# Two groups of a block product share the matmul loop, and consecutive matmuls go to their two PSUM banks in turn

## Time and profile before

| | |
|---|---|
| median of 3 runs | 984.03 us (983.54 to 985.64) |
| the profiled execution | 983.49 us, of which its span in the profile is 981.7 us |
| TensorE matmuls (PE) | busy 976.0 us, 99% of the span, 4786 instructions |
| TensorE weight loads (PEld) | 806.6 us, 82% |
| VectorE (DVE) | 799.4 us, 81% |
| ScalarE (ACT) | 406.6 us, 41% |
| GpSimd (POOL) | 37.0 us, 4% |
| granted TensorE clock, mean | 0.999 |

### The profile page before, as it was taken

One profiled execution on the slowest core, in us unless ns is written; L12 is line 12 of the kernel. 1 busy time (PEld: TensorE's weight loads), 2 busy tenths in 40 slices (PEclk: granted clock), 3 DMA queues, 4 the chain that ended last, 5 costly groups with the idle time before them and its releaser, 6 DMA issues.

```text
span 981.7 us, 12530 instructions
## 1 busy us (share of the span) xinstructions
PE 976.0 (99%) x4786; PEld 806.6 (82%) x4786; DVE 799.4 (81%) x644; ACT 406.6 (41%) x373; POOL 37.0 (4%) x63
## 2 busy tenths in 40 slices
PE   9999999999999999999999999999999999999998
PEld 7888888888888888888898888888888888888886
DVE  3977877998967897778867788779987779897887
ACT  5553563443345333332355545444334453423312
POOL 2700000000000000000100000000000000000001
PEclk9999999999999999999999999999999999999999
DMA  9022035024112101240531210620340131012013
GB/s 351 15 86 108 1 134 208 18 70 169 48 44 96 76 1 65 81 177 0 189 155 42 87 43 6 229 109 25 119 158 1 43 129 44 1 64 86 1 44 129
DMA packets 23274, 84.69 MB, mean 86 GB/s; under 512 B 2722, under 2 KB 6834, under 8 KB 17330
## 3 DMA queue, kind: packets, MB, share of 16 engines
q1 hardware_dynamic: 20962, 76.03, 21.4%
q0 software_dynamic: 2112, 7.36, 1.9%
q10 hardware_dynamic: 144, 0.52, 0.2%
HBM read 75.51 MB, written 8.39 MB: 85 GB/s over the span
## 4 chain that ended last, share of the span: by engine, by line
PE 98%; DMA 1%; SPq 0%; DVE 0%; issue 0%
PE banks L697 31%; PE banks L698 31%; PE banks L699 31%; PE banks L789 2%; PE banks L753 1%; DMA r<-x_pairs_in 1%; PE banks L772 1%; SPq L549 0%; SPq L579 0%; PE banks L802 0%; PE banks L818 0%; DVE r L1089 0%; SPq L529 0%; PE banks L812 0%; SPq L504 0%
## 5 line engine op out<-in xcount | busy, mean ns | idle before, releaser
L697 PE MATMUL banks<-s_hi,t_hi 128*128 128x512 f32 x1344 | 525.4, 391 | 0.0
L698 PE MATMUL banks<-s_lo,t_hi 128*128 128x512 f32 x1344 | 523.1, 389 | 0.0
L699 PE MATMUL banks<-s_hi,t_lo 128*128 128x512 f32 x1344 | 523.0, 389 | 0.0
L697 PEld LDWEIGHTS banks<-s_hi,t_hi 128*128 128x128 f32 x1344 | 252.3, 188 | 54.6 <-issue 1.5
L699 PEld LDWEIGHTS banks<-s_hi,t_lo 128*128 128x128 f32 x1344 | 252.3, 188 | 52.6
L698 PEld LDWEIGHTS banks<-s_lo,t_hi 128*128 128x128 f32 x1344 | 252.4, 188 | 51.4
L958 DVE TENSOR_TENSOR t_lo<-w,t_hi 128x1024 fp32r<-128x1024 f32 x134 | 159.9, 1218 | 8.7 <-ACT t_hi L891 8.7
L1084 DVE TENSOR_TENSOR r<-banks,r 128x1024 f32<-128x1024 f32 x102 | 123.5, 1219 | 46.3 <-PE banks L699 39.8
L891 ACT CAST t_hi<-w 128x1024 fp32r<-128x1024 f32 x134 | 136.5, 1048 | 51.3 <-PE banks L699 42.3
L863 ACT CAST s_hi<-st 128x2048 fp32r<-128x2048 f32 x40 | 76.5, 1913 | 182.8 <-PE banks L699 130.4
L958 DVE TENSOR_TENSOR s_lo<-st,s_hi 128x2048 fp32r<-128x2048 f32 x40 | 91.6, 2291 | 46.0 <-ACT s_hi L863 46.0
(11 more groups left out here) (84 smaller groups left out, 428.2 us busy)
## 6 DMA issues: line engine op xcount, KB each, us to landing
w<-w_up_in SPq DMA_DIRECT2D x16, 1024.0 KB, 4.8
w<-w_base_in SPq DMA_DIRECT2D x10, 1024.0 KB, 4.9
w<-w_down_in SPq DMA_DIRECT2D x8, 1024.0 KB, 5.0
r<-x_t_in SPq DMA_DIRECT2D x8, 1024.0 KB, 6.3
w<-w_lin_in SPq DMA_DIRECT2D x8, 1024.0 KB, 5.2
out_t<-r POOLq DMA_DIRECT2D x14, 512.0 KB, 4.1
we<-w_expin_in SPq DMA_DIRECT2D x10, 512.0 KB, 4.6
r<-x_pairs_in SPq DMA_DIRECT2D x8, 512.0 KB, 9.8
```

Source lines behind the costliest of these rows:

```text
L697: pe.matmul(out, w_hi, x_hi, start=start, stop=False, skip_group_check=True)
L698: pe.matmul(out, w_hi, x_lo, start=False, stop=False, skip_group_check=True)
L699: return pe.matmul(out, w_lo, x_hi, start=False, stop=stop, skip_group_check=True)
```

## The change

Groups are taken in pairs (0, 1), (2, 3), (4, 5). Within a pair the loops run over chunks, over the three forms (0: hi*hi, 1: hi*lo, 2: lo*hi), and innermost over the two groups: consecutive matmuls use the same activation columns, other weights, and the two groups' banks in turn. The number of matmuls, their operands and, in each bank, their order stay as they were. All waits of the pair stand ahead of its first matmul: the bank of the odd group is waited for there too. The even group is signalled done by its last matmul, which is the last but one of the pair. The products of exp with i = 3, 4, 5 keep the old order. Nothing on the other engines is changed.

```diff
-            def product(n, g, p, start, stop):
+            def product(n, g, p, form, fresh):
                 out = banks[:, bank_of(n, g), :]
...
-                pe.matmul(out, w_hi, x_hi, start=start, stop=False, skip_group_check=True)
-                pe.matmul(out, w_hi, x_lo, start=False, stop=False, skip_group_check=True)
-                return pe.matmul(out, w_lo, x_hi, start=False, stop=stop, skip_group_check=True)
+                x = (s_lo if form == 1 else s_hi)[:, slot, cols]
+                return pe.matmul(out, w, x, start=fresh and form == 0, stop=form == 2 and p == chunks_in(n) - 1,
+                                 skip_group_check=True)
...
-                for g in range(groups_in(n)):
+                for first in range(0, groups_in(n), 2):
+                    pair = (first, first + 1)
+                    if kind == "exp" and i in (3, 4, 5):
+                        for g in pair:
+                            pe.wait_ge(s_ready, n + 1)
+                            pe.wait_ge(t_ready, t_at(n, t_half_of(n, g)))
+                            wait_bank_free(n, g)
+                            for p in range(chunks_in(n)):
+                                for form in range(3):
+                                    last = product(n, g, p, form, (g >= 4 or i == 5) and p == 0)
+                            last.then_inc(group_done, 1)
+                            route(n, g)
+                        continue
                     pe.wait_ge(s_ready, n + 1)
-                    pe.wait_ge(t_ready, t_at(n, t_half_of(n, g)))
-                    wait_bank_free(n, g)
-                    fresh = g >= 4 or i in (0, 1, 5)
-                    begun = lora and g >= 2
+                    pe.wait_ge(t_ready, t_at(n, t_half_of(n, first)))
+                    wait_bank_free(n, first)
+                    wait_bank_free(n, first + 1)
+                    fresh = first >= 4 or i in (0, 1, 5)
+                    begun = lora and first == 2
                     for p in range(chunks_in(n)):
-                        last = product(n, g, p, fresh and p == 0 and not begun, p == chunks_in(n) - 1)
-                    if lora and g == 1:
+                        for form in range(3):
+                            for g in pair:
+                                last = product(n, g, p, form, fresh and p == 0 and not begun)
+                                if p == chunks_in(n) - 1 and form == 2 and (not lora or first == 2):
+                                    last.then_inc(group_done, 1)
+                    if lora and first == 0:
                         pe.wait_ge(lora_ready, lora_count(n))
                         pe.wait_ge(t_ready, t_at(n, LORA))
                         wait_bank_free(n, 2)
                         wait_bank_free(n, 3)
                         lora_out(n)
-                    elif not lora or g >= 2:
-                        last.then_inc(group_done, 1)
-                    if kind == "exp":
-                        route(n, g)
```

More of the change, by code:

```diff
@@ L689, in tensor_engine @@
         def tensor_engine(pe):
-            def product(n, g, p, start, stop):
+            def product(n, g, p, form, fresh):
                 out = banks[:, bank_of(n, g), :]
                 at, slot = ((g * 2 if kind_of(n) == "expup" else g % 2 * 4) + p) * P, T_ID[n, t_half_of(n, g)] % 4
-                w_hi, w_lo = t_hi[:, slot, at:at + P], t_lo[:, slot, at:at + P]
+                w = (t_lo if form == 2 else t_hi)[:, slot, at:at + P]
                 slot, cols = s_place(n)
                 cols = slice(cols.start + p * TN, cols.start + (p + 1) * TN)
-                x_hi, x_lo = s_hi[:, slot, cols], s_lo[:, slot, cols]
-                pe.matmul(out, w_hi, x_hi, start=start, stop=False, skip_group_check=True)
-                pe.matmul(out, w_hi, x_lo, start=False, stop=False, skip_group_check=True)
-                return pe.matmul(out, w_lo, x_hi, start=False, stop=stop, skip_group_check=True)
+                x = (s_lo if form == 1 else s_hi)[:, slot, cols]
+                return pe.matmul(out, w, x, start=fresh and form == 0, stop=form == 2 and p == chunks_in(n) - 1,
+                                 skip_group_check=True)
             def wait_bank_free(n, g):
```

## The result

| | before | after |
|---|---|---|
| median us (22 runs each) | 983.43 (982.83 to 985.64) | 984.56 (983.77 to 988.25) |
| the profiled execution, us | 983.49, span 981.7 | 986.54, span 984.8 |
| DVE busy, us | 799.4 | 798.7 |

The ratio after to before is 1.0014, 95% interval 1.0008 to 1.0020: slower by 1.1 us, inside the forecast's "no change" of 0.2%. The forecast time is 0.04 us off, and that closeness is luck: the sum behind it left out about half of the loss, and started from a median that was 0.6 us too high, as will be seen. The profiled execution after the change is 2 us above its kernel's median, so a part of its span is not the change's.

A forecast was written before the change was run, and what follows sets the result against it. PE's own instruction chain bounds the kernel: 4032 matmuls at 226.7 ns, 914 of 981.7 us. Terms 0 + 0 + 0 + 0.6 us on 983.49 gave 984.1, plus 0.54 to the median: 984.6 us, range 982.9 to 986.6.

The forecast's parts named there:

- Banks in turn: Large matmuls on PE: alternating banks leaves the 226.7 ns spacing as it is; 0 us, bounds -48 and +23 us.
- Rival 1: Large matmuls: same-bank overhead of 13.4 ns is real and alternation lifts it; 48 us faster, 936 us; chance 0.05.
- rival 2: Large matmuls: alternation has a price per matmul, 6.3 ns at 233 ns spacing; +23 us, 1007 us; chance 0.04.
- Rival 3: PE's clock: gaps from alternation lower it to 1.2 GHz; a tenth of 3600 matmuls costs 77 us, 1061 us; chance 0.02.
- Weights changed at every matmul: Lines 697 and 698, neighbours sharing weights: separating them loses nothing, since the load is issued for 698 anyway; 0 us.
- Waiting for both banks ahead of the pair: Start of each pair: odd bank needed 2.7 us sooner (expup 1.4), covered by at least 5.4 - 2.7 us; 0 us.
- The even group is signalled 11 matmuls later: Readers of the even group: signal 2.5 us later (expup 1.1 us); sum +0.6 us, bounds +0.4 and +1.3.
- (a): "addb" and "gate" adds on DVE: second of a pair ends 0.65 us later, hidden; 16 us at the very worst.
- (b): LORA slot refill by ACT: starts about 2.5 us later, next s_lo slips about 1 us; lead 7.4 us, hidden.
- (c): Last product: group 3's add starts 0.42 us later behind group 2's, its store costs 0.2 us more.
- The tightest place: Expup, product 83: t_lo ends at 972.59, its matmul starts at 972.74; nothing moves, but there is no cover.
- Rival 4: Expup: uncovered DVE chain turns late, 0.65 us in each of five tight products, twice; 6.5 us, 991 us; chance 0.03.

The follow-up runs named there:

- m1: Changed kernel plus nine blocks of 48 matmuls behind the last product, varying banks, weights, width and type; some 100 us longer, spacing 226.7 ns in two and four banks.
- e1: Changed kernel with groups 2 and 3 of lin's product 6 one after the other as before; median 983.83 us, ratio 1.0008 to the kernel before.
- e5: Kernel before, old order; only in lin's product 6 is group 2 signalled together with group 3; median 984.30 us, ratio 1.0009 to the kernel before.
- e4: Kernel before, old order; even groups signalled together with the odd ones, except in exp's products 3, 4, 5; median 984.97 us, ratio 1.0017.

## Why the prediction was right, and where it was not

*Banks in turn, 0 ns: right.* The reading of the group borders in the earlier trace rows held for steady alternation: 16.32 us for 72 spacings, and m1 has the same spacing in one, two and four banks. Rival 1 (936 us) and rival 2 (1007 us) fell on that. The argument from the number of borders in two stages forecast it rightly, and m1 showed it. Rival 3 (the clock) fell as well: the granted clock was at its full level over the whole stream of large matmuls, and its one fall lay ahead of the first of them.

*The Trainium skill's figure* ("TensorE: Matmul & The Clock Gate", Back-to-back issue gap: N / 2.4 + 2.5 ns, 216 ns for 512 columns) is met by the bf16 blocks of m1, 216 ns, and not by the fp32r matmuls, 226.7 ns. The section calls it the gap of an isolated matmul and holds it for too large in a stream; in the streams of m1 the mean spacing is never below it. So the 10.9 ns that I weighed were there, but they go with the operands' type and not with the bank.

*Weights changed at every matmul, 0 us: right.* One block repeated 48 times is no faster than 32 different ones.

*Waiting for both banks ahead of the pair, 0 us: right where PE does not stand, as e1 shows, and 0.11 us short at each stall.* At the one place where PE did stand, both banks are freed by one add, so the wait ends at the same moment as in the old order; but the matmul starts 0.256 us after the add and not 0.147. That is 2 x 0.11 = 0.22 us of the loss. My cover, "at least 5.4 - 2.7 us", did not look at this place: before the change it was 2.4 us.

*The even group is signalled 11 matmuls later.* (a) "addb" and "gate": hidden, as said; no stall in up0, up1 or down. (b) **The refill of a LORA slot is the step that failed.** I wrote of DVE's next s_lo that it would "slip by about 1 us", against a lead of 7.4 us. That was one such slot, in the middle of lin, and there it came out as said: t_lo starts 2.47 us later, the 1.22 us that DVE idled behind it before the change are used up, the next s_lo is 1.17 us late, and no matmul waits. But I took this one slot for all and followed the lag no further. The slot of lin's product 6 is refilled for exp, where DVE goes 25 us without idle time over 0.11 us; a lag of 2.3 to 2.5 us travels through its list to an add on which PE depends with 2.4 us to spare. The term was 0.48 us, not 0; e1 and e5 show that this slot's signal opens the stall, and the second bank wait makes 0.22 us of it. (c) The last product: mechanism right, size 0.47 us against 0.6. The add came 0.38 us later (0.42 foreseen), and the store cost 0.1 us more, not 0.2.

*The tightest place*, did not move, as said.

*Sum.* 0.6 us predicted, from the tail alone; 0.95 us measured in the traces, 0.47 of tail and 0.48 of stall, and 0.9 to 1.1 us in the medians. So the loss was half as large again as forecast, or more. That the forecast time, 984.6 us, is so close to the measured 984.56 is luck: the median of the first three runs, from which it was reckoned, was itself 0.6 us above that of all 22, and this made up for the term left out. From 983.43 the same sum would have given 984.0. Rival 4 named the kind of thing that happened (a dependence turned late) but at the wrong place, in expup, and with more than ten times the price.

## What to carry to other kernels

Before alternating banks, look in the trace at the borders where the bank already changes: here two stages with different numbers of borders took the same time for the same matmuls, and there was nothing to win. When a group's end is signalled later, follow each waiter to where it acts and then down its engine's list as long as that has no idle time: here the lag was paid 25 us on. Count the waits in a row at such a place, since each takes time of its own once the engine stands. In the last group of a kernel keep results coming one after the other, since two that end together queue behind each other. And before a difference of two traces is put down to a change, compare the granted clock window by window.

## What the runs showed of the hardware

Adding to a bank just written costs nothing: 226.7 ns for 512 columns and 120 ns for 256, in one bank as in two (blocks of 48 matmuls). Over the columns at 2.4 GHz (213.3 and 106.7 ns) that is 13.3 ns for each fp32r matmul at either width, where bf16 has 2.5 ns. What in the 4-byte operands makes it was not taken apart; that weights of 64 columns are slightly slower (230 ns) than those of 128 speaks against the length of the weight load.

When PE stands for a bank that an add on DVE frees, the matmul starts 0.147 us after the add's end with one wait ahead of it (four stalls, e4 and e5) and 0.256 us with two (five of six stalls of the pair's order; the sixth 0.346).

In the start of one execution the granted clock was 0.57 between 9 and 13 us, after PE had been idle for 2.01 us, and the start took 1.6 us longer for it; after 1.81 us of idle time in another execution it stayed at 1.00.

And the busy time of a group of matmuls depends on which neighbours share its line and form: it fell by 97 us for each form here, with nothing faster.
